# Causal attention with four PSUM banks for scores and three for maxima, turned outputs through the scores' ring, and values in bursts of two groups

## The reference

```
scores = einsum('bqhd,bkhd->bhqk', Q, K) / sqrt(8)
scores = where(causal, scores, -inf)
attn   = softmax(scores, axis=-1)
out    = einsum('bhqk,bkhd->bqhd', attn, V).reshape(B, S, 128)
return out @ W_o
```

## Time and profile before

| | us |
|---|---|
| median of 3 runs | 1352.45 (1351.22 to 1353.58) |
| profiled execution, its own time | 1351.48 |
| span of the profiled execution, first to last instruction | 1349.7 |
| mean granted TensorE clock | 0.967 |
| busy: PE, DVE, ACT, POOL | 1225.1, 1112.1, 922.2, 760.5 |
| causal attention, first maximum to last copy of psO | 67 to 574 |

### The profile page before, as it was taken

The page is one execution under the profiler, slowest core; times in us unless marked ns, Lnnn a source line. Parts: engine busy times, 40 slices in busy tenths (PEclk is TensorE's granted clock), DMA queues, the critical chain, the costliest instruction groups (busy, mean ns, idle before and its releaser), DMA issues. The chain is left out here.

```text
span 1349.7 us, 30205 instructions
## 1 busy us (share of the span) xinstructions
PE 1225.1 (91%) x10501; PEld 705.7 (52%) x10501; DVE 1112.1 (82%) x2911; ACT 922.2 (68%) x2463; POOL 760.5 (56%) x770
## 2 busy tenths in 40 slices
PE   6389999999999999888899999799899999997895
PEld 3223434434443443356566666565466766665663
DVE  5488998998999898689899999766598999997675
ACT  6316776777777677578888888433588888885344
POOL 5212212332331233478999999532699999997244
PEclk9759999999999999999999999899999999998998
DMA  5430121112112101011111111100112111111001
GB/s 142 143 128 6 45 60 47 59 51 64 39 39 60 47 13 35 25 41 41 32 31 34 33 33 33 41 1 1 24 32 48 33 33 33 29 29 25 1 17 47
DMA packets 36286, 56.45 MB, mean 42 GB/s; under 512 B 6931, under 2 KB 23709, under 8 KB 33821
## 3 DMA queue, kind: packets, MB, share of 16 engines
q1 hardware_dynamic: 35440, 54.29, 15.0%
q10 hardware_dynamic: 696, 0.25, 0.1%
HBM read 27.78 MB, written 8.39 MB: 27 GB/s over the span
## 5 line engine op out<-in xcount | busy, mean ns | idle before, releaser
L1137 ACT ACTIVATE a_prob<-a_psE 128x512 f32<-128x512 f32 (+1 forms) x608 | 303.1, 591 | 134.5 <-PE a_psE L749 133.0
L1539 DVE CUSTOM_DVE_ANT_0 a_psM<-a_psM,mask_q 128x384 f32<-128x384 f32 (+3 forms) x512 | 234.6, 523 | 40.9 <-PE a_psM L733 40.3
L733 PE MATMUL a_psM<-a_ks,a_qs 72*128 72x512 bf16 (+3 forms) x768 | 241.3, 343 | 20.9 <-PEq L106 17.2
L1372 POOL TENSOR_SCALAR_AFFINE_SELECT a_prob<-a_prob 128x512 f32<-128x512 f32 x128 | 80.8, 638 | 309.3 <-ACT a_prob L1137 305.6
L749 PE MATMUL a_psE<-a_qs,a_ks 84*128 84x512 bf16 (+3 forms) x768 | 238.3, 333 | 12.1 <-ACT a_prob L1137 6.5
L1431 POOL TENSOR_TENSOR w_rn<-w_ssm,mhalf 128x16 f32<-128x16 f32 x64 | 220.5, 3445 | 50.8 <-DVE w_ssm L1631 35.5
L1247 ACT ACTIVATE w_prob<-w_psS,w_bias 128x128 f32<-128x128 f32 x512 | 180.3, 378 | 21.2 <-DVE w_bias L1657 21.1
L1416 POOL TENSOR_TENSOR w_t<-w_raw,w_sin 128x256 f32<-128x256 f32 x252 | 176.5, 732 | 0.0
L1541 DVE TENSOR_REDUCE a_nm<-a_psM 128x1 f32<-128x512 f32 x256 | 158.8, 682 | 14.9 <-PE a_psM L733 14.0
L1421 POOL TENSOR_TENSOR w_rot<-w_t,w_t 128x1024 f32<-128x1024 f32 x63 | 148.6, 2358 | 8.7 <-issue 0.4
L749 PEld LDWEIGHTS a_psE<-a_qs,a_ks 84*128 84x128 bf16 x768 | 74.5, 98 | 147.6 <-ACT a_prob L1137 76.2
(11 more groups left out here) (189 smaller groups left out, 2426.0 us busy)
## 6 DMA issues: line engine op xcount, KB each, us to landing
a_qs<-q_parts SPq DMA_DIRECT2D x16, 576.0 KB
a_ks<-k_parts SPq DMA_DIRECT2D x16, 576.0 KB
q_parts<-p_parts SPq DMA_DIRECT2D x24, 128.0 KB
k_parts<-p_parts SPq DMA_DIRECT2D x24, 128.0 KB
w_vb__719<-w_v__703 SPq DMA_DIRECT2D x16, 128.0 KB, 2.2
w_vb__720<-w_v__703 SPq DMA_DIRECT2D x16, 128.0 KB, 2.3
w_vb__720<-w_v__704 SPq DMA_DIRECT2D x16, 128.0 KB, 2.2
w_vb__721<-w_v__704 SPq DMA_DIRECT2D x16, 128.0 KB, 2.3
```

What stands on the lines that cost most here:

```text
L733: mm = pe.matmul(psM[:, m_bank(r), at:at + n], qs[0:ROWS, g, j, i * P:(i + 1) * P], ks[0:ROWS, g, j, 512 * kc:512 * kc + n], start=True, s ...
L1137: act.activation(prob[G % NPROB][:, j - share + 1:j + 1, 0:w], psE[:, r % NRING, 0:share * w].rearrange("p (j n) -> p j n", j=share), ACT. ...
L1539: d = dve.tensor_tensor_reduce(scores, scores, sb["mask_q"][:, 512 - n:512], -1.0, -3.0 * NEG, ALU.add, ALU.min, low)
```

## The change

- psE gets four banks and psM three. e_bank(r) and e_ring(r) give the bank and the depth of the scores' ring; from group LAST_G - 11 on it narrows to three, as one of its banks is used by the window layers' values. A wait is added in front of project_v(0).
- Turned outputs (turn_outputs) go to the scores' ring, except the last three (in_tail). ACT gets a new step, compact(e, qc), which copies the 16 x 9 values that are wanted out of each turned bank into o_sum in SBUF, at n = 4 and n = 8 after everything else of that group. DVE's outputs(e, qc) reads o_sum instead of psM, one group later (n = 5 and n = 9), and counts in a semaphore of its own (o_made), for which turn_o waits.
- values of two groups at n = 1, 3, 5, 7, 9, 11, in place of two at n = 1, 3, 5 and three at n = 8 and 11.
- o_sum lies in the last batch's part of the tile xf, for which reason xf is allocated last.

```
-VALUES_BEHIND = {1: (3, 2), 3: (3, 2), 5: (3, 2), 8: (4, 3, 2), 11: (4, 3, 2)}
+VALUES_BEHIND = {n: (3, 2) for n in range(1, NGR, 2)}
...
+def in_tail(e, qc):
+    return (e, qc) >= (NSTAGE - 2, 1)
...
+E_NARROW = E_SLOT["s", LAST_G - 11, 0] // 4 * 4
 def m_bank(r):
-    return r % 4 if r < M_TAIL else 2
+    return r % 3 if r < M_TAIL else 2
+def e_bank(r):
+    return r % 4 if r < E_NARROW else 1 + (r - E_NARROW) % 3
+def e_ring(r):
+    return 4 if r < E_NARROW else 3
...
-        NPROB, NRING, MRING = 5, 3, 4
+        NPROB, MRING = 5, 3
...
-                    ge(pe, e_read, r - NRING + 1)
-                mm = pe.matmul(psE[:, r % NRING, j % share * w:(j % share + 1) * w], ks[0:KROWS, g, j, kt * P:(kt + 1) * P], qs[0:KROWS, g, j, q0:q0 + w],
+                    ge(pe, e_read, r - e_ring(r) + 1)
+                mm = pe.matmul(psE[:, e_bank(r), j % share * w:(j % share + 1) * w], ks[0:KROWS, g, j, kt * P:(kt + 1) * P], qs[0:KROWS, g, j, q0:q0 + w],
...
             def turn_outputs(e, qc):
                 pe.wait_ge(o_copied, 2 * e + qc + 1)
+                if in_tail(e, qc):
+                    r = o_slot(e, qc)
...
+                else:
+                    r = E_SLOT["o", e, qc]
+                    ge(pe, e_read, r - e_ring(r) + 1)
+                    out, done = psE[:, e_bank(r), :], e_ready
...
             def turn_o(b, h):
-                pe.wait_ge(m_read, o_slot(NG * b + NG - 1, h) + 1)
+                if b < B - 1:
+                    pe.wait_ge(o_made, 2 * (NG * b + NG - 1) + h + 1)
+                else:
+                    pe.wait_ge(m_read, o_slot(NG * b + NG - 1, h) + 1)
...
                 if G == LAST_G - 9:
+                    pe.wait_ge(e_read, E_NARROW - 3)
                     project_v(0)
...
+            def compact(e, qc):
+                r = E_SLOT["o", e, qc]
+                act.wait_ge(e_ready, r + 1)
+                ge(act, o_made, 2 * (e - 1) + qc + 1)
+                act.activation(o_sum[:, qc, :, :], psE[:, e_bank(r), :].rearrange("p (n c) -> p n c", c=32)[:, :, 0:VA], ACT.Copy).then_inc(e_read, 1)
...
             def outputs(e, qc):
...
+                else:
+                    ps = o_sum[:, qc, :, :]
+                    dve.wait_ge(e_read, E_SLOT["o", e, qc] + 1)
...
-                        if G >= 0 and o_turn_group(e, qc) == G:
+                        if G >= 0 and o_turn_group(e, qc) == (G if in_tail(e, qc) else G - 1):
                             outputs(e, qc)
```

More of the change, by code:

```diff
@@ L388, in m_slots @@
             for qc in range(2):
-                if o_turn_group(e, qc) == G:
+                if o_turn_group(e, qc) == G and in_tail(e, qc):
                     slots["o", e, qc] = n
@@ L444, in e_slots @@
                     n += 1
+        for e in range(max(0, G // NGR - 1), G // NGR + 1):
+            for qc in range(2):
+                if o_turn_group(e, qc) == G and not in_tail(e, qc):
+                    slots["o", e, qc] = n
+                    n += 1
     return slots, n
@@ L609, in attend_and_layers @@
             psM = banks.enter_context(nc.psum_tensor("a_psM", [P, MRING, 512], F32))
-            psE = banks.enter_context(nc.psum_tensor("a_psE", [P, NRING, 512], F32))
+            psE = banks.enter_context(nc.psum_tensor("a_psE", [P, 4, 512], F32))
         psEb = psE[:, :, :].bitcast(BF16)
@@ L799, in turn_o @@
                     r = E_SLOT["t", b, h]
-                    ge(pe, e_read, r - NRING + 1)
-                    out, done = psE[:, r % NRING, :], e_ready
+                    ge(pe, e_read, r - e_ring(r) + 1)
+                    out, done = psE[:, e_bank(r), :], e_ready
                 for t in range(4):
@@ L1163, in copy_turned @@
                 act.wait_ge(e_ready, r + 1)
-                act.activation(to, psE[:, r % NRING, :], ACT.Copy).then_inc(e_read, 1)
+                act.activation(to, psE[:, e_bank(r), :], ACT.Copy).then_inc(e_read, 1)
             def copy_projected(b, h):
@@ L1329, in _ @@
                 mix_step(G)
+                for s in range(max(0, e - 1), e + 1):
+                    for qc in range(2):
+                        if o_turn_group(s, qc) == G and not in_tail(s, qc):
+                            compact(s, qc)
             copy_raw(2)
@@ L1959, in latent_attention_and_window_layers @@
         }
+        sb["xf"] = tile("xf_sb", [P, NT, D])[:, :, :]
+        sb["last_xf"] = nc.sbuf_base - TB * D * 4
         tile("arena", [P, ARENA // 4])
```

44 lines of the change are left out of this document (23 added, 21 removed).

## The result

| | before | after |
|---|---|---|
| median, us | 1352.56 (1351.22 to 1353.58) | 1363.06 (1359.54 to 1364.19) |
| ratio to before, 95% interval | | 1.0074 [1.0053, 1.0094] |
| profiled execution, its own time and its span | 1351.48, 1349.7 | 1362.59, 1360.8 |

The change makes the kernel 0.7% slower. The forecast was 1361, slower. The page of after answers to the earlier trace rows. The counts of instructions are the same except for ACT's 29 small copies; PE is listed as busy for 8.5 us more with the same 10501 matmuls, in a run whose mean granted clock is 0.961 instead of 0.967.

A forecast was written before the change was run, and what follows sets the result against it. Within a stage the bound was taken to change between DVE's pace, ACT's in n = 7 and 8, and PE's bursts. 1351.48 + 9.1 from fourteen stages = 1360.6; median 1.0 higher, taken as 1361; 8-in-10 range 1345 to 1369.

The forecast's parts named there:

- Gap behind n = 7: New burst of 1024 columns after 384-wide units: stock 1.33 against 2.80 needed, so DVE idle 1.5 us.
- n = 9: 0.6: Burst of 1024 columns behind n = 9: stock 2.5 against 3.1 needed, DVE idle 0.6 us where none was.
- n = 3: 0.8: Burst of 896 columns behind n = 3: stock 2.0 against 2.8 needed, DVE idle 0.8 us.
- n = 11: 0.4 and n = 5: 0.2: DVE idle 0.4 us at the n = 11 burst (about 0.1 before) and about 0.2 at n = 5.
- Outputs 0.07 shorter each from SBUF: DVE's four output operations a stage, reading SBUF: 0.07 us less each, -0.2 a stage, bounds 0 to -0.3.
- ACT's copies: Two compact copies a stage on ACT, 0.6 us beside 7.6 of room; 0.6 a stage at most if uncovered.
- Rival D: Copies make ACT late in n = 4 to 8: +0.6 a stage, 1361; chance 0.53 together with the forecast.
- Score ring: Three to four score banks end PE's waits in n = 7 and 8; bounds 0 to -1.8, taken as 0.
- Mix stages: The three stages with mix steps, outputs included: +0.3 (30.69), +0.9 (30.04), +0.6 (29.33).
- I keep it: In the 30.69 stage, its 1.46 us of idle time beyond the plain stage's was carried over unchanged.
- Fourteen stages: All stages but first and last: four stages +2.6, times 3.5, +9.1 us.
- Ends: First stage 0 to +2, last stage 0 to -1.5, nothing taken for both together; window layers not touched.

The follow-up runs named there:

- e1: The changed kernel with the rings put back to four maxima and three score banks, turned outputs and bursts as changed; 1353.86 us.
- e3: The kernel before with only the maxima ring cut to three banks, the fourth left unused; 1375.38 us.
- e6: The changed kernel with a scores' ring of three banks, one left unused, maxima ring still three; 1371.31 us.
- e2: The kernel before with only the bursts changed, to two groups at n = 1, 3, 5, 7, 9, 11; 1354.77 us.
- e4: The changed kernel run again unchanged, for a second profile and time; 1360.97 us.
- e5: The changed kernel with the old bursts, three groups at n = 8 and 11; 1367.99 us.
- e7: The kernel before with only the turned outputs moved to the scores' ring and ACT's copy, old rings and bursts; 1356.63 us.
- e8: e1 with values of one group each at n = 6 to 9; 1353.72 us.
- e9: e1 with the bursts put later, behind n = 8 to 11; 1356.02 us.
- e10: The kernel before with the same later bursts, rings and turned outputs as they were; 1356.39 us.

## Why the prediction was right, and where not

The kernel is slower, by the mechanism forecast: the ring of three is short of stock at the bursts (e1, e3 and e6 show it), and the score bank does not pay for it. The size is right only in part. The plain stage takes 28.26, with DVE idle for 2.78; the forecast's own sign was 28.6 to 28.9 and an idle time near 3.3.

- *Gap behind n = 7: forecast 1.5, measured 1.28.* PE's side was right (2.80 forecast from the last unit's matmul to DVE's start, 203.07 to 205.84 measured, 2.77). The stock was 1.49, not 1.33: a series of masked units ends with the 0.14 of its last DVE_READ_ACCUMULATOR, which the pace of 0.51 leaves out. The reason given for the gap is only half of it, though: e1 and e2, with four maxima banks and three score banks, have 1.36 and 1.37 there, where PE behind ACT had no more than three banks in use at the burst. In the plain stage the ring of three shows behind n = 9 and n = 3.
- *n = 9: 0.6, measured 0.59; n = 3: 0.8, measured 0.65.* *n = 11: 0.4 and n = 5: 0.2, measured at most 0.10 each.* Together with the first, and some small ones, this makes 2.78 of idle time for the 3.5 forecast.
- *The gap behind n = 8 goes, and PE's waits change sides.* Both as forecast.
- *Outputs 0.07 shorter each from SBUF: wrong, nothing.* Lines of after from 70 to 850 us (busy us, mean ns, idle before), to set beside the earlier trace rows:

```profile
L1608 DVE TENSOR_TENSOR o_tok<-a_osum,a_rec 128x128 f32<-128x128 f32 x29 | 8.5, 292 | 1.0
...
L1603 DVE RECIPROCAL a_rec<-a_osum 128x16 f32<-128x16 f32 x29 | 7.2, 248 | 0.0
```

```profile
L1189 ACT ACTIVATE a_osum<-a_psE 128x144 f32<-128x144 f32 x29 | 9.2, 316 | 0.3
```

  292 and 248 ns against 291 and 248 from PSUM. The row of 174 ns was of another operation, and the difference lay in that: the reciprocal takes 248 from SBUF too. The Trainium skill's cycle table ("VectorE: DVE Perf Modes", TRN2 errata) would have made each 0.065 us shorter; these rows do not agree, and the measurement decides.
- *ACT's copies: 0.6 a stage, hidden.* 2 x 0.316, and no wait of PE or DVE in after names them. Rival D is out.
- *Score ring: 0.* The -1.8 in four stages that e6 shows is what the forecast's full maxima ring took for granted: with three score banks PE, held by ACT, does not fill it (e6's plain stage 28.76 against 28.26, PE's loads of scores waiting 4.3 us for ACT against 1.7). The Trainium skill's remark that a repeated gap can mean too few buffers ("Perfetto Trace Analysis", Identifying Performance Opportunities) holds for both rings here: 4.0 for the one, 1.8 for the other, per four stages. It could not have said which.
- *Mix stages: +0.3, +0.9 and +0.6 forecast; -0.44, +1.10 and +0.50 measured.* The last two came out; the stage with project_o has 3.59 of idle time, as forecast (3.6). The failed step is in the first, "I keep it". Its additional 1.46 contained the 0.28 by which turn_o made the gap behind n = 8 longer (2.08 against 1.80), and I counted turn_o once more, as 0.3, at the new burst of n = 7. That gap, of before and then of after:

```profile
236.60 0.70 DVE L1539 CUSTOM_DVE_ANT_0 a_psM<-a_psM,mask_q 128x512 f32<-128x512 f32 x1 [2.08 <-PE a_psM L733]
```

```profile
236.09 2.48 DVE L1584 TENSOR_REDUCE a_nm<-a_psM 128x1 f32<-128x512 f32 x4 [1.72 <-PE a_psM L757]
```

  Of the 0.8 by which the forecast's 4.5 of idle time exceeds the 3.67 measured, 0.2 are this, and 0.6 are the gaps of the plain stage other than n = 3's, put at 2.7 and measured at 2.13. Of the -0.44 only -0.27 is idle time; the other -0.17 is DVE's busy time, in no term of the forecast and not followed up.
- *Fourteen stages: +9.1 forecast, +4.75 measured.* This is the term that was mis-sized, almost by half: the plain stage was put at +0.8 and measured +0.29, the stage with turn_o as above. The fourteen hold five plain stages and three of each other kind, not three and a half sets; with that count the forecast's own terms give +9.4, so the weights are not the reason.
- *Ends: 0 forecast.* The first stage costs 1.2, inside the 0 to +2 that I gave, with the lower clock named above in it. The end of the attention costs 1.3 to 2.2 where I had 0 to -1.5; the same stretch takes 38.9 to 42.1 in the kernels above without a pattern that I can name, and its cause stays open. The mean granted clock of that stretch is 0.96 in before, 0.92 in after and 0.96 in e4, so the clock can have to do with the 0.9 between after and e4, but not with the 1.3 of e4. The window layers' 2.7, clock, was in no bound.

So 1360.6 was forecast for the profiled execution, 1362.6 came, from 4.3 too much inside the stages and 6.4 too little outside them. The sign was earned, the closeness partly luck.

## What to carry to other kernels

Price each ring by itself before swapping buffers: here one bank was worth 4 to 5.6 us in four stages in one ring and 1.8 in the other. A burst on the feeding engine costs the reader what it lasts beyond the stock, and small work of the reader beside the burst (the outputs at n = 8) is stock too: moving it moves the gap. What splitting a burst is worth hangs on what else stands there: nothing in the kernel before (e2), 0.95 in four stages with three maxima banks (e5 to after), 2.1 where the outputs had left the burst bare (e7 to e1). Splitting further (e8) or moving bursts (e9, e10) won nothing, because the queue of the feeding engine stood behind a third engine.

## What was unexpected of the hardware

- The same window layers take 774.6 to 775.4, 776.7 or 777.6 us, as three stretches of half clock make 17, 20.5 or 24 us together; each comes as 3.4, 6.8 or 10.2 us or not at all, in kernels whose code is the same there.
- DVE's operations on 16 and 128 elements a partition take the same from SBUF as from PSUM (248 and 292 against 248 and 291 ns); ACT's copy of 144 columns out of PSUM takes 316 ns, and 286 for 128 columns on 64 partitions.
- A series of masked maxima ends 0.14 us behind its pace, by the last read of the accumulator.
